# Relation rows: PE reads the places of sixteen pairs in one register load instead of eight

## What is computed

```python
h_proj = jnp.einsum('nd,rde->rne', h, relation_weight)
t_r = h_proj[etype, src]
h_r = h_proj[etype, dst]
att = jnp.sum(t_r * jnp.tanh(h_r + efeat), axis=-1)
```

## Time and profile before

| | |
|---|---|
| median of three runs | 7777.89 us (7766.84 to 7782.8) |
| span of the profiled execution | 7865.6 us; no other time of this execution is given |
| instructions | 104440 |
| busy shares of the span | PE 55%, weight loads 44%, DVE 61%, ACT 30%, GpSimd 47% |
| stage of the relation rows | from 195.6 to 1430.6 us of the span |
| granted TensorE clock there | mean 0.52 of full speed, which is its lower level, 1.2 GHz, in most of it |

### The profile page before, as it was taken

How to read it: one execution, slowest core, us unless ns; L and a number is a source line. 1 busy time by engine, 2 the same in 40 slices (tenths; PEclk the granted TensorE clock), 3 DMA queues, 4 the chain that set the end, 5 groups by cost and what they waited for, 6 DMA issues and landing times. The chain is left out here.

```text
span 7865.6 us, 104440 instructions
## 1 busy us (share of the span) xinstructions
PE 4297.8 (55%) x26852; PEld 3458.2 (44%) x26923; DVE 4772.7 (61%) x7334; ACT 2362.7 (30%) x3661; POOL 3733.3 (47%) x4217
## 2 busy tenths in 40 slices
PE   5777777310279545555535444444695444444397
PEld 2677776310179545555523222222683222222396
DVE  4666666688521156566547666666665766666675
ACT  5444444117322145555522111111222111111121
POOL 3666566100200166666625555553654555655363
PEclk9555555555589777777767666666896766666696
DMA  8677777895578533233225656564654666656462
GB/s 313 191 219 212 222 203 226 228 236 191 215 250 307 183 112 115 96 117 114 91 72 147 159 152 156 154 157 119 135 134 114 157 158 155 160 150 158 100 140 75
DMA packets 1472089, 1296.30 MB, mean 165 GB/s; under 512 B 1257993, under 2 KB 1297567, under 8 KB 1459038
## 3 DMA queue, kind: packets, MB, share of 16 engines
q1 hardware_dynamic: 902378, 671.59, 28.5%
q0 software_dynamic: 167008, 441.69, 21.0%
q10 hardware_dynamic: 402580, 181.62, 8.4%
HBM read 942.23 MB, written 351.27 MB: 164 GB/s over the span
## 5 line engine op out<-in xcount | busy, mean ns | idle before, releaser
L2503 POOL DMA_INDIRECT rows_p<-node_rows,stage_i x1632 | 1546.5, 948 | 1228.0 <-issue 978.9
L2557 PE MATMUL psZ<-parts_r,hot_t 128*128 x4896 | 1164.3, 402 | 1360.5 <-DVE lz L2638 867.7
L2557 PEld LDWEIGHTS psZ<-parts_r,hot_t 128*128 128x128 bf16 x4896 | 590.0, 121 | 1938.6 <-issue 1624.4
L2646 DVE TENSOR_TENSOR psZ<-psZ,rows_p 128x1320 f32<-128x1320 f32 x408 | 626.5, 1536 | 768.9 <-remote 283.0
L731 POOL DMA_INDIRECT rows_s<-hpx,hpST x784 | 741.4, 946 | 486.4 <-issue 203.8
L1961 POOL DMA_INDIRECT both<-table,srcI x784 | 741.9, 946 | 431.5 <-issue 211.1
L749 PE MATMUL psP<-window,pair_hot 128*128 x3136 | 701.9, 416 | 249.0 <-ACT pair_hot L771 146.6
L749 PEld LDWEIGHTS psP<-window,pair_hot 128*128 128x128 f32 x3136 | 672.8, 325 | 279.2 <-issue 279.0
L828 DVE SCALAR_TENSOR_TENSOR pair_run<-pair_run,same_c,psP 128x64 f32<-128x64 f32 x1568 | 440.2, 281 | 469.1 <-PE psP L749 209.1
L2953 PE MATMUL ps_steps<-A,xs 128*65 128x125 f32 x5184 | 578.8, 272 | 137.8 <-DVE A L2971 93.1
L2638 DVE SCALAR_TENSOR_TENSOR lz<-psZ,att 128x1320 f32<-128x1320 f32 (+2 forms) x428 | 642.6, 1501 | 8.4
(11 more groups left out here) (545 smaller groups left out, 7260.0 us busy)
## 6 DMA issues: line engine op xcount, KB each, us to landing
tile<-adj SPq DMA_DIRECT2D x168, 781.2 KB, 4.9
xs<-x_src SPq DMA_DIRECT2D x432, 128.0 KB
x_src<-rows_p SPq DMA_DIRECT2D x204, 256.0 KB
hpx<-stage ACTq DMA_DIRECT2D x25, 2048.0 KB
window<-hpx SPq DMA_DIRECT2D x196, 256.0 KB
dst_runs<-pair_run SPq DMA_DIRECT2D x28, 1792.0 KB
eaT<-in_ea SPq DMA_DIRECT2D x28, 1792.0 KB
adj<-tile SPq DMA_DIRECT2D x42, 781.2 KB
```

What stands on the lines that cost most here:

```text
L2503: pool.indirect_dma_start(rows[:, k, j, :], None, g.node_rows, bass.IndirectOffsetOnAxis(stage[:, k, j:j + 1], 0)).then_inc(got[k], 16)
L2557: last = pe.matmul(psZ[:, n % 2, j, 0:ZH], hot[:, k, col * CE:(col + 1) * CE], parts[:, bass.ds(at[col], 1), q, :].rearrange("p o c -> p ( ...
L2646: v.tensor_tensor(here, here, rows[:, slot, at * G:(at + 1) * G, 0:ZH], ALU.add).then_inc(added, 1)
```

## The change

Before an even batch PE loads sixteen places, those of this batch and the next, which lie side by side in the table; the odd batch takes the second half of the registers and loads nothing. `n` is the batch in the turn, a constant of the unrolled body.

```diff
                     for n in range(2 * M):
                         k, m = divmod(n, M)
-                        rel = nc.values_load_multi_w_load_instructions(
-                            g.pair_rel[0:1, bass.ds(batch(i, n) * BP, BP)], engines=[mybir.EngineType.PE], min_val=0, max_val=BP - 1,
-                            skip_runtime_bounds_check_because="bounded where the table is made")[1]
+                        if n % 2 == 0:
+                            both = nc.values_load_multi_w_load_instructions(
+                                g.pair_rel[0:1, bass.ds(batch(i, n) * BP, 2 * BP)], engines=[mybir.EngineType.PE], min_val=0, max_val=BP - 1,
+                                skip_runtime_bounds_check_because="bounded where the table is made")[1]
+                        rel = both[n % 2 * BP:(n % 2 + 1) * BP]
                         pe.wait_ge(window_in[n % 2], i * (16 * M) + (n // 2 + 1) * 16)
                         pe.wait_ge(hot_ready, batch(i, n) + 1)
```

## The result

The change cost a little. Over 20 runs the median is 7784.4 us, against 7774.4 us of the kernel before in the same series; the ratio is 1.0017, with a 95% interval of 1.0010 to 1.0024. Between the medians lie 10 us; the ratio says 13, its interval 8 to 19.

The account below looks back on a forecast made before the run. PE was taken as fullest but held by waits, its sequencer mattering only where late. Batch 12's 0.8 us a turn made 11 us, other terms zero: 7778 to 7789 us; 8-in-10 range 7757 to 7825.

Parts of the forecast that it names:

- Where the cost comes from: Longer loads ahead of even batches, mostly behind sixteen short tile products with less cover; 1.3 to 4.2 us a turn at PE.
- The price of a load of sixteen: Register loads ahead of even batches: 1.11 us for sixteen values, 0.52 more than for eight; 1.89 times if traffic slows each value.
- the flat 0.5: Lower case for the longer loads: traffic holds up a load only once, so each grows by 0.52 us.
- 0.8 us a turn for batch 12: Batch 12's delay, passed on in full: middle of 0.52 to 1.09 us a turn, giving 11 us in all.
- The removed loads are worth nothing: Odd batches' loads end 1.5 us or more ahead of need, so removing seven a turn gains nothing.
- That all delay ahead of batch 12 passes on: No gap behind batch 12, so its delay reaches the end in full: 7 to 15 us in all.
- That batch 4's delay goes into the gap behind it: Batch 4's 1.65 us delay goes into PE's 1.71 us wait for batch 5's window, so nothing reaches the end.
- the whole delay passes on: Rival: no gap absorbs PE's delay, stage 58 us longer, 7836 us; with half of it 7807; chance 0.23.
- That batch 2 has room: Batch 2's load ends 2.7 us before its products, so its growth of 0.52 us stays within its room.
- 312 us for nothing that the profile names: PE's idle time ahead of the pair products, 312 us, without a cause named by the profile.
- the rival of the removed loads: Rival: the removed odd loads were on the path; a fifth of 105 us counts, 21 us less, 7757; chance 0.13.
- What the profile after would show: 98 loads of at least 1.1 us, gaps ahead of batches 12 and 4, smaller gap ahead of 5, stage 1242 to 1250 us.

Follow-up runs that it names:

- the second series: The change and the unchanged kernel before run again on another chip, median of before 7829 us: ratios 1.0017 and 0.9999.
- the dose: Kernel before with two more loads of sixteen ahead of batch 12 alone: ratio 1.0039, 31 us over before.
- the first pair of profiles: Profiled executions of the kernel before and of the change: 7866 and 7789 us, possibly from different chips.
- the half that only removes: Kernel before with the odd batches' loads removed, using the places of the batch before them: ratio 1.0000.
- The small dose: Kernel before with one more load of eight ahead of batch 4 alone: ratio 1.0018, 14 us over before.
- the large one: Kernel before with two more loads of sixteen ahead of batch 4 alone: ratio 1.0053, 41 us over before.
- the early loads: Loads issued between the pair and tile products of an earlier batch, against the kernel before: 0.9979 with sixteen or eight values; eight again on another chip, 0.9997.
- both halves of the change: Against the kernel before: only longer even loads, odd loads kept, 1.0028; only odd loads removed, 1.0000.

## Why the prediction held, and which steps did not

The forecast was 11 us slower, 7789 for 7778, called no measurable change; measured are 10 us between medians, 13 by the ratio. The number and its direction were right. The path to it, all at batch 12 and nothing at batch 4, was right only in part.

**Where the cost comes from** was right: the longer loads cost 19 us by themselves where the removal brought nothing, and PE's idle time grew ahead of batches 2, 4 and 12, which come behind sixteen short tile products.

**The price of a load of sixteen** was right where nothing is in the way: 1.11 us by the line through 587 and 848 ns, 1102 measured. With traffic it was right at batch 4 (1.87 to 3.74 us in the mean of fourteen turns of the second series: twice), and too high at batch 12, where the growth was 1.28 to 1.85 us, that is the flat 0.5; that the longer load outlives the burst there is a guess which no run tests. The forecast's 0.8 us a turn for batch 12 was mis-sized: its idle time rose by 8.2 us in all, 0.6 a turn, and with the nine tenths of the dose that is some 7 us; in the first pair of profiles it rose by 4.2. One row of before spoke for a high price and was not weighed: beside SyncE's 1172 ns for fourteen values stood 3027 ns, in the median, for the same load on ACT. PE's own row was the one to go by.

**The removed loads are worth nothing**: shown, within 7 us, by the half that only removes, on the faster chip. In the trace of before none of the 98 odd loads ended less than 0.5 us ahead of its products. On the slower chips the removal was not tried.

**That all delay ahead of batch 12 passes on**: nearly, 31 of 35 us, with 19 to 42 as the interval.

**That batch 4's delay goes into the gap behind it** is the step that failed. It was read from one turn and taken for fourteen. The small dose passed 14 of 27 us, the large one 41 of 75. The same holds for batch 10, where the prediction counted on a gap of 6.54 us ahead of batch 11: in four turns of that trace there is none. The rival "the whole delay passes on" had named this mechanism with 58 us as its size; about a fifth of that was seen.

**That batch 2 has room** was read from the same one turn, and failed too. In the trace of before its load was the last thing to arrive in six turns of fourteen, ending 0.44 us ahead of the products, and with sixteen values it grew not by 0.52 but from 1.86 to 3.02 us in the mean of the second series.

**"312 us for nothing that the profile names"** added the weight loads' idle time to the matmuls'. The matmuls' own is 33 us, and the rival of the removed loads, which leaned on the 312, had that much less to stand on.

**The sum** hit the number by luck: the term for batch 12 was too high, and the terms for batches 4, 10 and 2 were set at zero and are not all zero. What was found in their place does not close either. By the doses batch 4 would give 11 to 14 us and batch 12 7, so 18 to 21 together, more than the 13 of the change; it is inside the second series' interval of 5 to 22, but for the most part above the first measurement's 8 to 19. And batches 2 and 10 were not tried apart: in the second series PE's idle time ahead of them rose by 14 and 8 us, and how much of it passes on stays open.

**What the profile after would show** came true in the loads (98, of 1102 ns at least, the longest 4765) and in the gap ahead of batch 4 with a smaller one behind it. The new gap ahead of batch 12 is 0.42 to 0.48 us in most turns, just under the 0.5 to 1 that was said. The stage was to last 1242 to 1250 us, and a shorter one was to be a sign against the forecast; the window shows 1234, 1 us shorter. That sign was finer than two profiles can tell apart.

Against the floor of about 600 ns that the Trainium skill gives for a register load (DMA: Bandwidth & Descriptors, Latency and other measured facts), the 587 ns for eight values looked like agreement. The page says of it that the compiler unrolls four times to amortize it; it doesn't say that a longer load costs the same. The 848 ns for twelve and the 1102 for sixteen show that from eight values on they are paid one by one, some 64 ns each; joining two loads of eight saves 2 x 587 - 1102 = 72 ns of sequencer time, and moves all the rest to the place with less cover. The Trainium skill's other rule, about 200 ns for each register even in bulk (Runtime: NRT & Kernel Launch, Instruction fetch mechanics), stands there among the loads that the runtime puts in; the table here lies in SBUF. By it sixteen values would make 3.2 us, an estimate from the page's figure; measured without traffic is a third of that.

## What to carry to other kernels

To price an instruction of the sequencer, look not at how long it takes but at how long before the next product it ends, at each place where it stands, and in many turns of the loop: a mean gap, or one turn's gap, does not tell how much delay the gaps take up. Merging two short register loads into a long one saved little here, 72 ns of 1174, since the values are read one by one. What helped on one chip was to move the load to a place where the longest matmuls are already queued ahead of it; there even the long load was free. On another chip the same move gained nothing.

## Not expected of the hardware

The same program takes 6827 us on one chip and 7774 to 7863 on the others, at 0.72 and 0.68 of the full TensorE clock in the mean. Single instructions take much the same time: a load of eight values takes at least 587 ns on either. The stage took 999 us there with the odd loads removed, which changes nothing, and 1222 here. The windows of the stage, first on the slower chip, then on the faster:

```profile
200.00:1420.00 1220.00, 921.58 (x5227) 881.93 (x5226) 755.10 (x1761) 569.33 (x682) 734.07 (x779) 0.50 0.73 212
```

```profile
203.00:1202.00 999.00, 877.31 (x5236) 855.44 (x5236) 752.01 (x1761) 578.60 (x685) 736.17 (x781) 0.53 0.90 259
```

The busy times hardly differ; the DMA engines are busy 0.90 of the time at 259 GB/s there, 0.73 at 212 here. On the slower chip PE stood idle for 5.2 to 6.5 us ahead of batch 11 in eleven turns of fourteen, in the four profiles of the faster one never; what makes the difference was not tried. It matters for this case, for the early loads gained 14 us on the one and nothing on another of the slower kind, and both halves of the change were tried on the faster chip alone.
